# Attention and feed-forward on one core: the place of VectorE's joining adds in a group of score maxima

## The chip, the cores and the metric

One Trainium2 core runs the whole program. The metric is the device time of one execution in microseconds (us); lower is better.

## The reference, cut to what matters

```
x  = hidden states, 2048 tokens x 512, fp32
xn = layernorm(x)
q, k, v = xn @ w_qkv.T, 16 heads of 32
p  = softmax(causal(q k.T / sqrt(32)))        # per head, 2048 x 2048
x + (p v) @ w_o.T + ffn(xn)                   # ffn: fp4 weights, gate/up/down, 4096 wide
```

The change lies in the softmax alone. Softmax needs, for every query row, the maximum of its scores first and the sum of its exponentials at the end.

## The kernel before, in words

The program has three stages: norm and projections, attention (about 165 to 725 us of the span), output projection and feed-forward. In each, every engine has its own instruction list, executed in order, and semaphores tie the lists together.

Attention takes the 16 heads as 8 pairs (p0 to p7). For a pair, the transposed scores are made in 40 steps (a chunk of 512 queries against 128 keys, for both heads), and four steps are a group: ten groups a pair, 80 in all. A group is called here by its first step in its pair: s0, s4, ..., s36. The last group of each query chunk (s0, s8, s20, s36) lies on the diagonal; the other six (s4, s12, s16, s24, s28, s32) lie off it.

In group k the engines do this:

- TensorE (PE) makes the transposed scores of the group after (`scores_t`, L1041), eight of them, and between them plain scores (`scores`, L1013), eight "units" for maxima that a later pair of heads needs. It then adds the sums of exponentials of the group before into `p_o` (`row_sums`, L1084; off the diagonal it waits for `joined`), multiplies the group's exponentials with V (`product_v`, L1067, 32 matmuls), and only then makes the eighth unit. The units go to a ring of four banks of `p_s`: `bank_free` makes PE wait until the maximum of the unit four places back in the ring is taken. In groups with a `turn_max` (L1023), that one takes a place in the ring between unit seven and unit eight.
- ScalarE (ACT) turns the transposed scores into exponentials in `e_sb` (L819).
- VectorE (DVE) takes the maximum of each unit: `unit_max`, L902 on whole tiles, L898 where the diagonal is masked; L898 leaves a short accumulator read behind it. After the last unit of a batch of rows it joins the parts in `row_max` (`join_parts`, L909). Groups have eight units up to the last pair; from s12 of the last pair on there are none.
- GpSimd (POOL) adds the exponentials of two steps into `e_sum` (L736), two heads by two pairs of steps: four adds a group off the diagonal. Its order in group k is: the last two adds of group k, the first two of group k + 1, then the splitting of a batch of row maxima into three bf16 parts (`split`, L751 to L759; it waits for `row_max`), then in some groups a `normalise` (L770, in s12, s16, s24 and s28 of pairs 2, 4 and 6, and of the last).
- Off the diagonal DVE then adds the two halves of those sums (`join_sums`, L957): one add for each head, 128x512 fp32, both inputs in SBUF. It first waits for POOL's four adds of the group. Two of the joined buffers come free with it: POOL's last two adds of the following group wait for `joined`, where that group is also off the diagonal.

DVE's order in a group, before:

```
for n in units:
    if n == units[-1]:
        join_sums(k)
    unit_max(n)
    ...join_parts where a batch of rows ends
sum_steps(k)
if not units:
    join_sums(k)
```

A batch of rows ends, and `join_parts` follows, behind the sixth unit in s8, s12, s20 and s32.

Of the kernel before, what the change touches and what calls it, by code (L numbers as in the profile page):

```python
# [348 lines left out]
def attention(nc, qk_scratch, v_scratch, sum_scratch, rsum_scratch, wo_t, wo_sb, attn_t, xn_hi, xn_lo, e_sb, wv_hi, wv_lo, p_v,  # L349
# [14 lines left out]
    S_BUFS = 4  # L364
# [37 lines left out]
    def units_of(k):  # L402
        return list(range(unit_end[k - 1] if k else FIRST, unit_end[k]))
# [18 lines left out]
    for k in range(NG):  # L422
        units = units_of(k)
# [10 lines left out]
    for k in range(NG):  # L434
        diag = DIAG[GS * k % NS]
        if diag:
            ADDS.append([(a, a, 1, 0) for a in range(2)] + [(a, a, i, None) for i in (2, 3) for a in range(2)])
        else:
            ADDS.append([(2 * j + a, a, 2 * j + 1, 2 * j) for j in range(2) for a in range(2)])
        first_sum.append(len(sum_group))  # L440
        sum_group += [k] * (2 if diag else 4)
        for i, (m, a, _, _) in enumerate(ADDS[k]):
            vector = not units_of(k) and (a == 1 if diag else m >= 2)
            by_vector += vector
            by_pool += not vector
            made[k, i] = (vector, by_vector if vector else by_pool)
        added_to.append((by_pool, by_vector))

    def used_up(g, a):
        k, j = divmod(g, GS)  # L450
        return made[k, max(n for n, (_, b, y, x) in enumerate(ADDS[k]) if b == a and j in (x, y))]
# [8 lines left out]
    with ExitStack() as ctx:  # L460
# [102 lines left out]
        def exps_for(k, i):  # L563
            _, a, y, _ = ADDS[k][i]
            return (GS * k + y) * PIECES + a + 1
# [320 lines left out]
        def _(dve):  # L886
# [3 lines left out]
            def unit_max(n):  # L890
                a, i, b, w = UNITS[n % NU]
                part = max_part[:, a, i, b:b + 1]
                dve.wait_ge(scored, n + 1)
                if b == i // 4:
                    m = MASKED_UNITS.index(n)
                    if m >= 2:
                        dve.wait_ge(maxed, MASKED_UNITS[m - 2] + 1)
                    nc.vector.tensor_tensor_reduce(out=masked_scores[:, m % 2, 0:w], in0=p_s[:, slot[n] % S_BUFS, 0:w],  # L898
                                                   in1=score_mask[:, W - w:], scale=1.0, scalar=NO_MAX, op0=ALU.add,
                                                   op1=ALU.max, accum_out=part).then_inc(maxed, 1)  # L900
                else:
                    nc.vector.reduce_max(part, p_s[:, slot[n] % S_BUFS, 0:w], AX.X).then_inc(maxed, 1)  # L902

            def join_parts(p, r):
                tiles = slice(4 * r, 4 * r + 4)
                dve.wait_ge(maxed, p * NU + UNITS_TO[r])
                if p:
                    dve.wait_ge(max_split, (p - 1) * TC + r + 1)
                nc.vector.reduce_max(row_max[:, :, tiles], max_part[:, :, tiles, 0:r + 1], AX.X).then_inc(row_maxed, 1)  # L909

            def invert_sums(p):
                dve.wait_ge(sums_loaded, 16 * (p + 1))
                if p:
                    dve.wait_ge(rsums_out, 16 * p)
                nc.vector.reciprocal(rcompact[:, :], compact[:, :]).then_inc(sums_inverted, 1)

            def divide(qc):

                p, c = PAIRS - 1, (PAIRS - 1) * TC + qc
                if qc == TC - 1:  # L920
                    dve.wait_ge(rows_done, NG)
                    o = p_o[:, :, :]
                else:
                    dve.wait_ge(o_copied, c + 1)
                    o = o_sb[:, c % 2, :, :]
                dve.wait_ge(maxed, NUNIT)
                if qc:
                    dve.wait_ge(divided, 4 * qc)
                nc.vector.reciprocal(recip[:, 0:HALF], o[:, 1, :]).then_inc(inverted, 1)
                dve.wait_ge(inverted, qc + 1)  # L930
                for a in range(2):
                    for h in range(2):
                        rows = slice((2 * a + h) * D, (2 * a + h + 1) * D)
                        nc.vector.tensor_tensor(attn_rows(p, a, qc)[:, h * HALF:(h + 1) * HALF], o[rows, 0, :],
                                                recip[rows, 0:HALF], ALU.mult).then_inc(divided, 1)

            def sum_steps(k):
                for i in range(len(ADDS[k])):
                    vector, count = made[k, i]
                    if vector:  # L940
                        dve.wait_ge(exp_done, exps_for(k, i))
                        free, earlier = needs(k, i)
                        if free:
                            dve.wait_ge(*free)
                        if earlier:
                            dve.wait_ge(vector_summed, earlier)
                        nc.vector.tensor_tensor(*operands(k, i), ALU.add).then_inc(vector_summed, 1)

            def join_sums(k):
                if DIAG[GS * k % NS]:  # L950
                    return
                dve.wait_ge(pool_summed, added_to[k][0])
                if added_to[k][1]:
                    dve.wait_ge(vector_summed, added_to[k][1])
                for a in range(2):
                    other, here = ((first_sum[k] + 2 * j + a) % SUM_BUFS for j in range(2))
                    nc.vector.tensor_tensor(e_sum[:, here, :], e_sum[:, here, :], e_sum[:, other, :],  # L957
                                            ALU.add).then_inc(joined, 1)
# [6 lines left out]
            for k in range(NG):  # L965
                p, s = divmod(GS * k, NS)
                if p and s == 8:
                    invert_sums(p - 1)
                units = units_of(k)
                for n in units:  # L970
                    if n == units[-1]:
                        join_sums(k)
                    unit_max(n)
                    for p_, r in BATCHES[k]:
                        if n + 1 == p_ * NU + UNITS_TO[r]:
                            join_parts(p_, r)
# [3 lines that stand above are left out]
                if p == PAIRS - 1 and s in (20, 24, 28):  # L980
                    divide({20: 0, 24: 1, 28: 2}[s])
                if 0 < k - LAST <= KT:
                    g = k - LAST - 1
                    dve.wait_ge(wo_hi_made, g + 1)
                    nc.vector.tensor_tensor(wo_lo[:, g, :], wo_sb[:, g, :], wo_hi[:, g, :].bitcast(F32),
                                            ALU.subtract).then_inc(wo_lo_made, 1)
# [671 lines left out]
```

## Time and profile before

| | |
|---|---|
| median of 3 runs | 1799.53 us (1797.9 to 1799.81) |
| the profiled execution | 1800.45 us, its span 1798.7 us |
| PE, DVE, ACT, POOL busy in the span | 1763.6, 1237.7, 715.2, 752.2 us |
| span of attention | about 165 to 725 us |

The times in the rows below are microseconds from the start of the span; "mean" columns are nanoseconds. A row of the timeline gives start, length, engine, line, operation, output<-input and the number of merged instructions, and in brackets the idle time of the engine in front and what ended it. Neighbouring instructions of DVE overlap by some 0.08 us, so a maximum of a whole tile that is listed with 0.68 us takes 0.60 us in a sequence.

### The profile page before, as it was taken

The numbers are of one execution on the slowest core, as the hardware profiler recorded it, in microseconds if no ns is written. First come the engines' busy times: TensorE is split into PE (matmuls) and PEld (weight loads), VectorE is DVE, ScalarE is ACT, GpSimd is POOL, SyncE is SP. The second block draws the span as 40 slices with busy tenths as digits, with TensorE's granted clock in tenths as the row PEclk, the third lists the DMA queues.
The fourth block names the chain that finished last, engine by engine and source line by source line (L and its number), as shares of the span: only waits on it lengthen the run. The fifth ranks groups of instructions, "written<-read, shape, count | busy, mean of one in ns | idle before, by whom it ended". The sixth has DMA issues, their size and how long they took to land.

```text
span 1798.7 us, 28378 instructions
## 1 busy us (share of the span) xinstructions
PE 1763.6 (98%) x10176; PEld 1346.1 (75%) x10176; DVE 1237.7 (69%) x1834; ACT 715.2 (40%) x1171; POOL 752.2 (42%) x716
## 2 busy tenths in 40 slices
PE   7999999999999999999999999999999999999998
PEld 6886666656556556888888888888888888888887
DVE  5526888888888889686676567567567666666654
ACT  3324666666666665233223232323233223222322
POOL 1432888888888886122122222222222222222221
PEclk9999999999999999999999999999999999999999
DMA  8775044144143111511110110110110010010002
GB/s 280 223 230 156 10 105 84 28 105 84 29 105 83 29 40 60 182 30 36 35 35 0 35 35 0 35 35 0 35 35 14 21 35 28 7 35 0 1 1 94
DMA packets 75615, 108.55 MB, mean 60 GB/s; under 512 B 24912, under 2 KB 44992, under 8 KB 72384
## 3 DMA queue, kind: packets, MB, share of 16 engines
q1 hardware_dynamic: 75520, 107.34, 22.1%
q8 instruction: 53, 0.87, 0.2%
q14 instruction: 42, 0.34, 0.1%
HBM read 74.04 MB, written 29.59 MB: 58 GB/s over the span
## 4 chain that ended last, share of the span: by engine, by line
PE 59%; DVE 0%; ACT 0%; issue 0%; ACTq 0%
PE p_up L52 7%; PE p_v L52 7%; PE p_up L51 7%; PE p_v L51 7%; PE p_up L50 7%; PE p_v L50 7%; PE p_s L51 6%; PE p_s L52 6%; PE p_s L50 6%; PE p_s L345 0%; PE p_s L339 0%; PE p_s L340 0%; PE p_v L339 0%; PE p_v L345 0%; PE p_v L340 0%; PE p_up L339 0%
## 5 line engine op out<-in xcount | busy, mean ns | idle before, releaser
L1392 POOL TENSOR_SCALAR poly<-poly 128x1024 f32<-128x1024 f32 (+1 forms) x65 | 72.4, 1114 | 800.8 <-ACT poly L1349 800.8
L736 POOL TENSOR_TENSOR e_sum<-e_sb 128x512 f32<-128x512 f32 (+1 forms) x244 | 304.4, 1271 | 75.5 <-ACT e_sb L819 39.1
L902 DVE TENSOR_REDUCE max_part<-p_s 128x1 f32<-128x512 f32 x384 | 247.1, 683 | 62.2 <-PE p_s L1013 61.3
L819 ACT ACTIVATE e_sb<-p_v 128x512 f32<-128x512 f32 (+3 forms) x427 | 216.1, 549 | 119.6 <-PE p_v L1041 59.1
L1455 DVE SCALAR_TENSOR_TENSOR inter<-inter,gate 128x1024 f32<-128x1024 f32 (+1 forms) x65 | 78.6, 1209 | 241.1 <-ACT inter L1355 240.3
L50 PE MATMUL p_v<-xn_hi,w_hi 128*128 128x512 f32 x512 | 199.2, 389 | 0.0
L51 PE MATMUL p_v<-xn_lo,w_hi 128*128 128x512 f32 x512 | 199.2, 389 | 0.0
L52 PE MATMUL p_v<-xn_hi,w_lo 128*128 128x512 f32 x512 | 199.2, 389 | 0.0
L50 PE MATMUL p_up<-xn_hi,w_hi 128*128 128x512 f32 x512 | 199.2, 389 | 0.0
L51 PE MATMUL p_up<-xn_lo,w_hi 128*128 128x512 f32 x512 | 199.2, 389 | 0.0
L52 PE MATMUL p_up<-xn_hi,w_lo 128*128 128x512 f32 x512 | 199.2, 389 | 0.0
L1348 ACT ACTIVATE gate<-p_v 128x1024 f32<-128x1024 f32 (+1 forms) x65 | 66.0, 1015 | 332.7 <-PE p_v L52 332.7
L50 PE MATMUL p_s<-stack_hi,w_hi 128*128 128x512 f32 x504 | 196.1, 389 | 0.0
L51 PE MATMUL p_s<-stack_lo,w_hi 128*128 128x512 f32 x504 | 196.1, 389 | 0.0
L52 PE MATMUL p_s<-stack_hi,w_lo 128*128 128x512 f32 x504 | 196.1, 389 | 0.0
L1395 POOL TENSOR_TENSOR poly<-poly,gate 128x1024 f32<-128x1024 f32 (+1 forms) x65 | 179.5, 2761 | 5.4
L1067 PE MATMUL p_o<-e_sb,v_stack 128*32 128x256 f32 (+1 forms) x2304 | 149.4, 374 | 0.0
L1355 ACT ACTIVATE inter<-poly 128x1024 f32<-128x1024 f32 (+1 forms) x65 | 68.1, 1047 | 202.3 <-POOL poly L1395 202.3
L1475 DVE TENSOR_TENSOR acc<-acc,p_s 128x2048 f32<-128x2048 f32 x63 | 143.7, 2280 | 3.3 <-PE p_s L52 3.3
L898 DVE CUSTOM_DVE_ANT_0 recip<-p_s,score_mask 128x128 bf16<-128x128 f32 (+3 forms) x256 | 115.8, 485 | 37.2 <-PE p_s L1013 36.4
L819 ACT ACTIVATE e_sb<-p_st 128x512 f32<-128x512 f32 (+2 forms) x213 | 117.3, 551 | 58.2 <-PE p_st L1041 30.3
L1360 ACT ACTIVATE stack_hi<-inter 128x1024 fp32r<-128x1024 f32 (+1 forms) x65 | 68.1, 1048 | 163.0 <-DVE inter L1461 163.0
(190 smaller groups left out, 3486.7 us busy)
## 6 DMA issues: line engine op xcount, KB each, us to landing
k_stack<-qk_scratch SPq DMA_DIRECT2D x42, 256.0 KB, 7.6
qk_scratch<-out_hi SPq DMA_DIRECT2D x32, 256.0 KB, 2.6
qk_scratch<-out_lo SPq DMA_DIRECT2D x32, 256.0 KB, 3.3
q_stack<-qk_scratch SPq DMA_DIRECT2D x24, 256.0 KB, 6.5
xn_lo_scratch<-xn_lo SPq DMA_DIRECT2D x4, 1024.0 KB, 5.2
v_stack<-in_gate_up_s SPq DMA_DIRECT2D x64, 64.0 KB, 2.3
xn_lo<-xn_lo_scratch SPq DMA_DIRECT2D x4, 1024.0 KB, 13.8
scales<-in_gate_up_s SPq DMA_DIRECT2D x64, 64.0 KB, 2.5
```

The lines of the kernel that those rows point to most:

```text
L50: nc.tensor.matmul(out, w_hi, x_hi, start=first, stop=False)
L51: nc.tensor.matmul(out, w_hi, x_lo, start=False, stop=False)
L52: return nc.tensor.matmul(out, w_lo, x_hi, start=False, stop=last)
L736: nc.gpsimd.tensor_tensor(*operands(k, i), ALU.add).then_inc(pool_summed, 1)
L819: nc.scalar.activation(e_sb[:, x % E_BUFS, 0:w], bank_st(x)[:, 0:w], ACT.Exp, scale=SCALE).then_inc(exp_done, 1)
L898: nc.vector.tensor_tensor_reduce(out=masked_scores[:, m % 2, 0:w], in0=p_s[:, slot[n] % S_BUFS, 0:w], in1=score_mask[:, W - w:], scale=1.0 ...
L902: nc.vector.reduce_max(part, p_s[:, slot[n] % S_BUFS, 0:w], AX.X).then_inc(maxed, 1)
L1067: last = nc.tensor.matmul(p_o[(2 * a + h) * D:(2 * a + h + 1) * D, 0, first - h * HALF:], v_stack[p % PB][:, kt, a, :], e_sb[:, (g * PIECE ...
L1392: nc.gpsimd.tensor_scalar(part_of(poly, h, parts), part_of(poly, h, parts), GELU_A, 1.0, ALU.mult, ALU.add).then_inc(poly_done, 1)
L1395: nc.gpsimd.tensor_tensor(part_of(poly, h, parts), part_of(poly, h, parts), part_of(gate, h, parts), ALU.mult).then_inc(poly_done, 1)
L1455: nc.vector.scalar_tensor_tensor(part_of(inter, h, parts), part_of(inter, h, parts), 1.0, part_of(gate, h, parts), ALU.add, ALU.mult).then ...
L1475: nc.vector.tensor_tensor(here, here, p_out[:, :, :], ALU.add).then_inc(added, 1)
```

## The change

DVE's two joining adds of a group off the diagonal stand in front of the fifth unit's maximum (`S_BUFS` is 4), where they stood in front of the last's. Groups on the diagonal have no joining adds, and groups without units keep theirs where they were. No operation is added or taken away.

```
--- before.py
+++ after.py
@@ -968,7 +968,7 360.18 0.44 PE L1013 MATMUL p_s<-k_stack,q_stack 96*128 96x384 f32 x1
...
427.50 0.45 PE L1013 MATMUL p_s<-k_stack,stack_lo 96*128 96x384 f32 x1
                     invert_sums(p - 1)
                 units = units_of(k)
                 for n in units:
-                    if n == units[-1]:
+                    if n == units[min(S_BUFS, len(units) - 1)]:
                         join_sums(k)
                     unit_max(n)
                     for p_, r in BATCHES[k]:
```

## Rows read from the trace of the kernel before

**Rows 1.** The page: busy time of the engines in the span.

```profile
PE 1763.6 (98%) x10176; PEld 1346.1 (75%) x10176; DVE 1237.7 (69%) x1834; ACT 715.2 (40%) x1171; POOL 752.2 (42%) x716
```

**Rows 2.** Groups of instructions, attention: the joining adds.

```profile
L957 DVE TENSOR_TENSOR e_sum<-e_sum 128x512 f32<-128x512 f32 x96 | 106.3, 1146 | 1.0 <-POOL e_sum L736 0.2
```

**Rows 3.** Waits in attention: engine line <- releaser: us, times, longest.

```profile
PEld p_s L1013 <- DVE max_part L902: 6.7, 16, 0.8
...
POOL e_sum L736 <- DVE e_sum L957: 5.2, 4, 1.3
...
PEld p_s L1013 <- DVE max_part L898: 4.5, 7, 0.9
...
PE p_s L1013 <- DVE max_part L898: 3.3, 7, 0.7
```

**Rows 4.** Timeline of DVE, pair 3, s12 and s16.

```profile
398.54 0.69 DVE L898 CUSTOM_DVE_ANT_0 recip<-p_s,score_mask 128x512 bf16<-128x512 f32 x1
...
399.88 0.17 DVE L909 TENSOR_REDUCE row_max<-max_part 128x8 f32<-128x8 f32 x1
...
400.56 1.32 DVE L957 TENSOR_TENSOR e_sum<-e_sum 128x512 f32<-128x512 f32 x2
...
404.15 0.69 DVE L902 TENSOR_REDUCE max_part<-p_s 128x1 f32<-128x512 f32 x1 [0.26 <-PE p_s L1013]
...
406.66 2.10 DVE L957 TENSOR_TENSOR e_sum<-e_sum 128x512 f32<-128x512 f32 x2
```

**Rows 5.** Timeline of POOL, pair 3, s12, s16 and (414 on) s20.

```profile
395.71 5.02 POOL L736 TENSOR_TENSOR e_sum<-e_sb 128x512 f32<-128x512 f32 x4
400.66 0.70 POOL L751 CAST max_cols<-row_max 128x8 bf16<-128x8 f32 x1
...
402.72 2.51 POOL L736 TENSOR_TENSOR e_sum<-e_sb 128x512 f32<-128x512 f32 x2
...
414.27 0.23 POOL L751 CAST max_cols<-row_max 128x8 bf16<-128x8 f32 x1
...
415.42 0.22 POOL L759 CAST max_cols<-rest 128x8 bf16<-128x8 f32 x1
```

**Rows 6.** Timeline of PE: the eighth unit of s16, pair 3.

```profile
408.58 0.50 PE L1013 MATMUL p_s<-k_stack,stack_lo 96*128 96x512 f32 x1
```

**Rows 7.** Timeline of POOL, pair 2, between s12 and s16.

```profile
334.75 1.28 POOL L770 TENSOR_TENSOR acc<-acc,rsum_rows 128x512 f32<-128x512 f32 x1
336.17 2.51 POOL L736 TENSOR_TENSOR e_sum<-e_sb 128x512 f32<-128x512 f32 x2
```

**Rows 8.** Timeline of DVE and of PE, pair 2, s16.

```profile
338.71 2.10 DVE L957 TENSOR_TENSOR e_sum<-e_sum 128x512 f32<-128x512 f32 x2
...
340.40 0.50 PE L1013 MATMUL p_s<-k_stack,q_stack 96*128 96x512 f32 x1
```

**Rows 9.** Timeline of DVE, s24 of pair 2, then s24, s28, s32 of pair 3.

```profile
350.08 1.89 DVE L902 TENSOR_REDUCE max_part<-p_s 128x1 f32<-128x512 f32 x3
351.89 3.45 DVE L957 TENSOR_TENSOR e_sum<-e_sum 128x512 f32<-128x512 f32 x2
...
418.27 1.89 DVE L902 TENSOR_REDUCE max_part<-p_s 128x1 f32<-128x512 f32 x3
420.08 1.66 DVE L957 TENSOR_TENSOR e_sum<-e_sum 128x512 f32<-128x512 f32 x2
...
426.33 3.23 DVE L957 TENSOR_TENSOR e_sum<-e_sum 128x512 f32<-128x512 f32 x2
...
434.38 2.33 DVE L957 TENSOR_TENSOR e_sum<-e_sum 128x512 f32<-128x512 f32 x2
```

**Rows 10.** Timeline of POOL, pair 3: first two adds of s32, during s28.

```profile
426.05 2.97 POOL L736 TENSOR_TENSOR e_sum<-e_sb 128x512 f32<-128x512 f32 x2 [1.60 <-PE p_o L1084]
```

**Rows 11.** Timeline of PE: the eighth unit of s28, pair 2, then pair 3.

```profile
360.18 0.44 PE L1013 MATMUL p_s<-k_stack,q_stack 96*128 96x384 f32 x1
...
427.50 0.45 PE L1013 MATMUL p_s<-k_stack,stack_lo 96*128 96x384 f32 x1
```

More of the change, by code:

```diff
@@ L970, in _ @@
                 for n in units:
-                    if n == units[-1]:
+                    if n == units[min(S_BUFS, len(units) - 1)]:
                         join_sums(k)
```

## The prediction

> **What bounds the kernel now.** The page first: PE is busy 98% of the span, DVE 69%, POOL 42% [rows 1]. The change touches attention only, so the question is what PE waits for there. The table of waits for that stretch says: units waiting for a maximum of DVE, 6.7 + 4.5 us in front of weight loads and 3.3 us in front of matmuls, 14.5 us in the listed rows; and POOL waiting 5.2 us, four times, for the joining adds [rows 3]. No wait of PE behind the joining adds stands there for groups with units: where they stand, in front of the eighth maximum, they use time in which DVE has nothing else, since PE makes the eighth unit only behind 32 product matmuls. The bound is a loop in which PE, ACT, DVE and POOL hand work round within about 7 us a group, and the timelines of single groups decide, not the shares.
>
> **What is moved.** Nothing is removed or added. 43 of the 48 groups off the diagonal have units, so 86 of the 96 joining adds move, from in front of the eighth maximum to in front of the fifth: the fifth, sixth and seventh maximum now come after the pair of adds, and with them `row_max` in s12 and s32. DVE waits in order, so three things count: is POOL done with its four adds when DVE gets there; how long does the pair take there; and who waits for the fifth, sixth and seventh maximum and for `row_max`.
>
> **The price of a pair.** The 96 adds average 1.15 us [rows 2], but a pair takes 1.32 us in s12, 1.66 in s24 of pair 3, 1.84 in s4, 2.10 in s16, 2.33 in s32, 3.23 in s28, 3.45 in s24 of pair 2 [rows 4, 8, 9]. The long ones run beside POOL's own adds, and POOL's two adds there take 2.97 us [rows 10] against 2.51 alone [rows 5]: they take turns. In s12 POOL's four adds from 395.71 on take 5.02 us: the last two of s12 to about 398.2, then the first two of s16 to 400.7 [rows 5]. Before, the pair came at 400.56, when POOL was through. After, it comes at 398.54, in the middle of them [rows 4, 5]. The bounds are 1.32 (its own row) and 3.45 us; I take 3.2, because the position matches s28's.
>
> [...]
>
> **s12 and s16, pairs without `normalise` (0, 1, 3, 5), by pair 3.** The pair of adds ends at 398.54 + 3.2 = 401.74. From the fifth maximum's start to the end of `row_max` it was 400.05 - 398.54 = 1.51 us [rows 4], so `row_max` is there at 403.25 instead of 400.05. Before, the split began at 400.66, behind POOL's adds. Now POOL stands idle until 403.35. A split takes, undisturbed, 415.64 - 414.27 = 1.37 us [rows 5]: 404.72. POOL's last two adds of s16 are queued behind it, 2.51 us: 407.23, against 405.23 before. In s16 DVE finished its fourth maximum at 404.84 before [rows 4], is about 1.4 us later now, and then waits for POOL until 407.23; the pair of adds takes 2.10 us as before (its second meets POOL's next ones): 409.33. The fifth maximum of s16 (256 columns and its accumulator read) 0.42 us: 409.75. The eighth unit reuses the bank of the fifth, since `turn_max` lies between: PE starts it at 409.75, not at 408.58 [rows 6]. That is 1.2 us, and all that stands behind on PE moves with it.
>
> **The same, pairs 2, 4, 6.** They run 408.58 - 340.40 = 68.18 us in front of their like in the next pair [rows 6, 8]. `row_max` at 403.25 - 68.18 = 335.07, split to 336.5, then `normalise`, 1.28 us and a gap of 0.14 [rows 7]: 337.9; two adds, 2.51: 340.4, against 338.7. Joining adds to 342.5, fifth maximum to 343.0: PE's eighth unit starts then, not at 340.40 [rows 8]: 2.6 us.
>
> **s24 to s36.** In pair 3 the pair of adds starts at 418.27 instead of 420.08, meets POOL's two adds for s28, takes 3.2 to 3.4 us and ends about 421.6; three maxima (1.81 us from 418.27 to 420.08) follow, to 423.4. The eighth maximum could start at 421.74 before, so it is 1.7 us late [rows 9]. The trace holds an experiment for that: pair 2's adds in s24 end at 355.34, which is 423.52 in pair 3's time, 1.8 us later than pair 3's, and PE's eighth unit of s28 is 360.18 + 68.18 - 427.50 = 0.86 us later [rows 9, 11]. Against this, in s32 the pair of adds should meet less of POOL's and fall from 2.33 to about 1.3 us. I take 0.9 us a pair of heads for 0, 1, 3 and 5. In pairs 2, 4 and 6 POOL is late in s24: the adds start 351.89, while the fourth maximum was through at 350.08, a wait of 1.8 us with nothing done in it, and the slack that pair 3 has is used up already [rows 9]. POOL's own lateness from s16 (1.7) is less than PE's (2.6), so some 0.9 of that wait goes. 1.0 us remains, and the shorter covers of s28 make it 1.2.
>
> **s4.** POOL is through long before, PE makes the eighth unit late: nothing. If the cover is gone, the pair's 1.84 us would be paid up to 0.3 us a time. The last pair has only its s4 with units. Diagonal groups: untouched.
>
> **Sum.** 4 x (1.2 + 0.9) + 3 x (2.6 + 1.2) = 8.4 + 11.4 = 19.8 us. The profiled execution took 1800.45 us, 0.9 above the median; on the median of 1799.53 this gives 1819.3, and I say 1819. Lower bound: the pair of adds keeps 1.32 us in s12 and 1.66 in s24; then only pairs 2, 4 and 6 lose, 338.68 + 2.10 + 0.42 - 340.40 = 0.8 and 1.0 us each, 5.4 in all: 1805. Upper bound: the split keeps its longer form (its first cast 0.70 us, the whole 2.06 from 400.66 to 402.72 [rows 5]), 0.7 more in seven pairs, the wait in s24 stays whole (0.9 in three), and 0.3 in 8 groups s4: 19.8 + 4.9 + 2.7 + 2.4 = 29.8: 1829.
>
> **Rivals.**
> *Faster.* The adds of s28 and s32 now hold back the eighth maximum, on which PE's fourth unit of the next group waits; and POOL waits 5.2 us for joined sums [rows 3]. With the adds forward, those buffers come free earlier, and in s32 they meet POOL less, 2.33 to 1.3 us in seven pairs: 7 us gained, 1792. It decides if in s12 the fifth maximum's delay stays under the wait for the eighth unit, that is, if the pair of adds there takes below about 2 us. Against it: POOL's adds lie right there [rows 5]. 0.10.
> *No difference.* PE makes the seventh unit without the fifth maximum, and waits for exponentials anyhow; the delays drown: 1799.5. For it: DVE is 69% busy. Against it: PE's eighth unit needs the fifth maximum in s16. 0.08.
> *Small loss.* The lower bound above, 1805; 0.17.
> *Forecast.* 1812 to 1829; 0.57.
> *Larger.* The delay of POOL is carried from group to group, so that s16, s20 and s24 all pay it: 2 us more in each of seven pairs, 1833 and above; 0.08.
>
> The range that leaves out most of "faster" and of "larger" is 1800 to 1832. About 0.2% (3.6 us) is what a measurement of this kernel can tell from no change: faster 0.10, same 0.08, slower 0.82.
>
> **What the profile after would show.** Joining adds (L957): more busy time than 106.3 us, by (3.2 - 1.32) x 7 and 1.6 x 4 less 1.0 x 7, about 119 us. In s12 a pair over 3 us; `row_max` over 3 us later there; a wait of POOL's L751 behind `row_max`, new in s12; a wait of DVE's L957 behind POOL's L736 in s16 and, in pairs 2, 4 and 6, in s24; a wait of PE's L1013 behind L898 in front of the eighth unit of s16. The feed-forward is unchanged. Wrong would be the prediction if the pair in s12 stayed at 1.3 us, if PE's eighth unit of s16 came as early as before, or if the waits fell below the 14.5 us of now.

## The result and the profile after

The kernel with the change takes 1814.34 us (median of 6, 1813.53 to 1815.21) against 1799.28 us before, a ratio of 1.0084 with a 95% interval of 1.0072 to 1.0096: 15.1 us slower. The prediction was 1819 us, 19.8 us slower, with a range of 1800 to 1832. (The change is the one line with `units[-1]`; in the diff under "The change", the two lines of PE with times are those of [rows 11].)

The page after, busy time of the engines, as in [rows 1]:

```profile
PE 1766.3 (97%) x10176; PEld 1347.7 (74%) x10176; DVE 1234.9 (68%) x1834; ACT 716.0 (39%) x1171; POOL 743.7 (41%) x716
```

The joining adds after, from the groups of instructions in attention, as in [rows 2]:

```profile
L957 DVE TENSOR_TENSOR e_sum<-e_sum 128x512 f32<-128x512 f32 x96 | 105.4, 1137 | 17.6 <-POOL e_sum L736 17.1
```

The waits after in attention, for [rows 3]:

```profile
POOL max_cols L751 <- DVE row_max L909: 44.7, 21, 20.1
...
PEld p_s L1013 <- DVE max_part L898: 20.0, 26, 2.8
...
DVE e_sum L957 <- POOL e_sum L736: 17.1, 10, 2.7
...
PE p_s L1013 <- DVE max_part L898: 12.0, 13, 2.3
PEld p_s L1013 <- DVE max_part L902: 11.5, 31, 0.6
...
POOL e_sum L736 <- DVE e_sum L957: 2.8, 4, 0.7
```

The adds take no more time in all than before (105.4 us for 106.3), but DVE now waits 17.1 us for POOL in front of them, where it waited 0.2. That is 1.08 us in s16 of pairs 0, 1, 3 and 5, 2.69 us in s16 and 1.56 to 1.59 us in s32 of pairs 2, 4 and 6; none of it is in s24. PE's waits for maxima grew: 4.5 to 20.0, 3.3 to 12.0 and 6.7 to 11.5 us. POOL waits 44.7 us for `row_max`, 26.4 before. POOL's wait for joined sums shrank from 5.2 to 2.8 us, and so did its wait for PE's row sums, from 30.0 to 18.5 us, since POOL comes later.

Pair 3 runs 4.8 us later than before when it begins, so 398.54 in [rows 4] answers to 403.37. DVE there, s12 and s16:

```profile
403.29 3.28 DVE L957 TENSOR_TENSOR e_sum<-e_sum 128x512 f32<-128x512 f32 x2
406.49 0.68 DVE L898 CUSTOM_DVE_ANT_0 recip<-p_s,score_mask 128x512 bf16<-128x512 f32 x1
...
407.82 0.17 DVE L909 TENSOR_REDUCE row_max<-max_part 128x8 f32<-128x8 f32 x1
...
411.87 1.29 DVE L957 TENSOR_TENSOR e_sum<-e_sum 128x512 f32<-128x512 f32 x2 [1.08 <-POOL e_sum L736]
```

POOL there, for [rows 5]:

```profile
401.78 4.24 POOL L736 TENSOR_TENSOR e_sum<-e_sb 128x512 f32<-128x512 f32 x3
408.05 0.22 POOL L751 CAST max_cols<-row_max 128x8 bf16<-128x8 f32 x1 [2.04 <-DVE row_max L909]
...
409.33 2.51 POOL L736 TENSOR_TENSOR e_sum<-e_sb 128x512 f32<-128x512 f32 x2
```

And PE: the second, third and eighth unit of s16, for [rows 6]:

```profile
407.84 0.33 PE L1013 MATMUL p_s<-k_stack,stack_lo 96*128 96x128 f32 x1 [0.28 <-DVE max_part L898]
408.64 0.50 PE L1013 MATMUL p_s<-k_stack,stack_hi 96*128 96x512 f32 x1 [0.47 <-DVE max_part L902]
...
414.38 0.50 PE L1013 MATMUL p_s<-k_stack,stack_lo 96*128 96x512 f32 x1
```

The pair in s12 takes 3.28 us, and `row_max` is 3.1 us late (407.82 for 399.88 + 4.83). POOL has a new wait of 2.04 us, its adds of s16 start 1.8 us late (409.33 for 402.72 + 4.83), and DVE waits for them. But PE is held up earlier, at the second and third unit of s16. Its eighth, 414.38 for 408.58 + 4.83 = 413.41, is 0.97 us late without a wait of its own.

DVE in s24, s28 and s32 of pair 3, and in s32 of pair 4, for [rows 9]:

```profile
423.97 2.98 DVE L957 TENSOR_TENSOR e_sum<-e_sum 128x512 f32<-128x512 f32 x2
...
431.15 1.27 DVE L957 TENSOR_TENSOR e_sum<-e_sum 128x512 f32<-128x512 f32 x2
...
437.36 1.28 DVE L957 TENSOR_TENSOR e_sum<-e_sum 128x512 f32<-128x512 f32 x2
...
510.06 2.10 DVE L957 TENSOR_TENSOR e_sum<-e_sum 128x512 f32<-128x512 f32 x2 [1.56 <-POOL e_sum L736]
```

Where the time went is told by the start of each group's first maximum on DVE, after less before, in microseconds:

| pair of heads | s0 | s16 | s20 | s24 | s28 | s0 of the next |
|---|---|---|---|---|---|---|
| 1 | 0.12 | 1.64 | 1.12 | 1.10 | 1.96 | 0.59 |
| 2 | 0.59 | 2.94 | 4.79 | 4.78 | 4.52 | 4.80 |
| 3 | 4.80 | 6.33 | 5.79 | 5.79 | 6.65 | 5.25 |
| 4 | 5.25 | 6.76 | 9.47 | 9.96 | 9.32 | 9.56 |
| 5 | 9.56 | 11.08 | 10.55 | 10.56 | 11.43 | 10.04 |
| 6 | 10.04 | 11.53 | 14.20 | 14.75 | 14.06 | 14.32 |

Pairs 0, 1, 3 and 5 lose 0.44 to 0.48 us each, 1.8 in all; pairs 2, 4 and 6 lose 4.2, 4.3 and 4.3 us, 12.8 in all. (0.8 us of pair 2's come in s8, where DVE waits 0.86 us for a DMA in front of the reciprocal of the sums; no other pair has this wait.) In pair 4, DVE and PE in s16, for [rows 8], one timeline each:

```profile
480.89 2.88 DVE L957 TENSOR_TENSOR e_sum<-e_sum 128x512 f32<-128x512 f32 x2 [2.69 <-POOL e_sum L736]
```

```profile
484.17 0.64 PE L1013 MATMUL p_s<-k_stack,q_stack 96*128 96x512 f32 x1 [2.31 <-DVE max_part L898]
484.60 0.63 PE L1041 MATMUL p_st<-stack_hi,k_stack 128*128 128x512 f32 x1
...
487.80 0.40 PE L1013 MATMUL p_s<-k_stack,q_stack 96*128 96x512 f32 x1
```

PE waits 2.31 us, and then its matmuls of 512 columns take 0.63 us instead of 0.40. Busy time by windows; the columns are the length and the busy time of PE, PEld, DVE, ACT and POOL, each with its count, then the granted clock, the share of the DMA engines and GB/s:

```profile
480.00:484.00 4.00, 1.85 (x36) 0.86 (x28) 3.11 (x3) 0.77 (x2) 3.77 (x4) 1.00 0.02 6
484.00:488.00 4.00, 3.83 (x10) 3.15 (x11) 3.09 (x11) 2.17 (x4) 3.87 (x6) 0.57 0.00 0
488.00:492.00 4.00, 4.00 (x51) 2.45 (x49) 2.91 (x8) 2.17 (x4) 3.08 (x8) 1.00 0.00 0
```

The granted clock was 0.57 in the mean of the window from 484 us: 0.5 of full speed for 3.4 us from 484.4 on, 1.00 on both sides. Pair 6 has the same 3.4 us at 0.5 in s16, from 624.3 on; pair 2, with a wait of PE of 2.30 us at the same place, has none.

### The profile page after: what moved, and what is told of

The parts are those of the page before. It is cut to its first block, busy times and chain, and to the rows that moved or that the text cites. A ratio compares the mean times of both kernels' runs of the same rounds, so it can differ in the third digit from the quotient of the medians.

```text
span 1812.9 us, 28378 instructions
## 1 busy us (share of the span) xinstructions
PE 1766.3 (97%) x10176; PEld 1347.7 (74%) x10176; DVE 1234.9 (68%) x1834; ACT 716.0 (39%) x1171; POOL 743.7 (41%) x716
## 4 chain that ended last, share of the span: by engine, by line
PE 59%; DVE 0%; ACT 0%; issue 0%; ACTq 0%
PE p_v L50 6%; PE p_up L50 6%; PE p_up L52 6%; PE p_v L52 6%; PE p_up L51 6%; PE p_v L51 6%; PE p_s L50 6%; PE p_s L52 6%; PE p_s L51 6%; PE p_s L340 0%; PE p_s L339 0%; PE p_s L345 0%; PE p_v L339 0%; PE p_v L340 0%; PE p_up L339 0%; PE p_v L345 0%
## 5 line engine op out<-in xcount | busy, mean ns | idle before, releaser
L736 POOL TENSOR_TENSOR e_sum<-e_sb 128x512 f32<-128x512 f32 (+1 forms) x244 | 308.4, 1289 | 78.3 <-ACT e_sb L819 55.7
```

Of the source, the lines that this page charges most:

```text
L736: nc.gpsimd.tensor_tensor(*operands(k, i), ALU.add).then_inc(pool_summed, 1)
```

## The experiments

In each kernel, a condition on the place of the joining adds selects groups; elsewhere they stand as before. Times of before in the same runs: 1799.33, 1798.68 and 1799.64 us for the three sets of runs. The gains and losses by group are read as in the table above, or, where PE is named, at the start of its units. The last pair has no joining adds moved behind s4, and yet its time differs from trace to trace: from its s8 on, e1, e4, e6 and e10 get 2.4 to 2.5 us back against before (in these four, its adds of s24 and s28 take 1.29 or 1.30 us each instead of 3.37 and 2.40), e5 and e8 1.2, e7 and e9 1.8, and after, e2 and e3 0.1 or less. So the losses of the pairs don't sum to the difference of the times.

**One group at a time, and the last three.**

```
-                    if n == units[min(S_BUFS, len(units) - 1)]:
+                    if n == units[S_BUFS if s == 12 else -1]:     # e1
+                    if n == units[S_BUFS if s == 16 else -1]:     # e2
+                    if n == units[S_BUFS if s >= 24 else -1]:     # e3
+                    if n == units[S_BUFS if s >= 28 else -1]:     # e4
```

*s12 alone (e1).* 

> The joining adds stand in front of the fifth maximum in s12 alone, elsewhere where they were. Theory A (two prices: the late maxima of s12 hold back PE's second to fourth unit of s16, 0.95 us in each of 7 pairs; the wait for POOL in s16 costs the rest): about +6.7 us, near 1806, PE 0.95 us later at s16 in every pair. Rival B (as predicted: all of it goes over the late row_max and POOL to the fifth maximum of s16, and only then to PE): with the adds of s16 in their old place nobody waits, 1799 to 1801.

Measured: 1806.07 us, ratio 1.004 (1.0026 to 1.0054), 6.7 us slower. The pair in s12 takes 3.25 to 3.28 us, and in every pair of heads PE comes 0.95 to 0.98 us late between the first and the eighth unit of s16, at the same place as above, though nobody waits for the joining adds of s16. (Pairs 2, 4 and 6 lose 0.9 us more in s20 and get 0.6 back in s24.) The place and the size at s16 are those of theory A; that the total agrees too is partly luck, since the pairs lose 7.9 us in the trace and the last pair gives 2.4 back. PE's second and third unit of s16, pair 3:

```profile
406.46 0.33 PE L1013 MATMUL p_s<-k_stack,stack_lo 96*128 96x128 f32 x1 [0.26 <-DVE max_part L898]
407.26 0.50 PE L1013 MATMUL p_s<-k_stack,stack_hi 96*128 96x512 f32 x1 [0.47 <-DVE max_part L902]
```

Rival B, the way that the prediction had given this delay, falls for these pairs.

*s16 alone (e2).* 

> The adds stand forward in s16 alone. Theory A: POOL is not later than before; pairs 0, 1, 3, 5 lose nothing, pairs 2, 4 and 6 wait about 2 us for POOL in front of the fifth maximum and PE's eighth unit is 0.8 us later there: +2.5 us, near 1802. Rival B says the same. Rival C (the wait in s16 is costly by itself, whatever s12 does): +9 us or more.

Measured: 1798.51 us, ratio 0.9996 (0.9987 to 1.0005), no difference, where +2.5 us was expected. The 0.82 us at the eighth unit of s16 is there in pairs 2, 4 and 6, and is given back in s28: POOL goes on while DVE and PE stand, so it is less late in s24, where the pair of adds now takes 2.57 to 2.62 us instead of 3.45.

*s24, s28 and s32 (e3).* 

> The adds stand forward in s24, s28 and s32. Theory A, read from the trace after (PE 0.5 us earlier from s24 to s36 in each pair): -3.3 us, near 1796. The prediction's term for these groups: +7.2 us, 1806.5.

Measured: 1807.3 us, ratio 1.0045 (1.003 to 1.0059), 8.0 us slower. Theory A was wrong for this one. The prediction's 7.2 us looks right, but not by its parts: pair 2 loses 1.81 us between s24 and s28, which is the wait for POOL that the prediction had priced at 1.8; pairs 2, 4 and 6 lose 2.1, 3.3 and 3.1 us in all, 4 and 6 with the granted clock at 0.5 of full speed for 3.4 and 6.8 us behind waits of PE of 1.72 and 1.70 us; pairs 0, 1, 3 and 5, priced at 0.9 us each, gain 0.1 us or less. That these groups cost nothing in the whole change goes with s12 and s16 having held DVE and PE up already: there DVE's wait in s24 is 0, here it is 1.81 us.

*s28 and s32 (e4).* 

> The adds stand forward in s28 and s32 only. Theory A: the pair in s24 keeps 1.66 us in pairs 0, 1, 3, 5, so their 0.3 us of loss at s28 goes: about -4.5 us, near 1795. If the short pairs of s28 (1.28 us in the trace after) come only because s24's adds are early, s28 keeps 3.2 us and the gain falls to 0 to -2 us.

Measured: 1808.88 us, ratio 1.0058 (1.0044 to 1.0072), 9.6 us slower, where -4.5 us was expected. Pairs 0, 1, 3 and 5 gain 0.8 us each (1.24 - 0.40 in pair 0) with both pairs of adds at 1.28 us. Pairs 2, 4 and 6 lose 5.6 us each. POOL is late in s28 there, so DVE waits for it 1.34 us and then takes 3.42 us beside its adds, PE waits 2.01 us, and the granted clock falls to 0.5. DVE, then PE, then windows of that kernel:

```profile
357.16 3.42 DVE L957 TENSOR_TENSOR e_sum<-e_sum 128x512 f32<-128x512 f32 x2 [1.34 <-POOL e_sum L736]
```

```profile
361.23 1.86 PE L1013 MATMUL p_s<-k_stack,q_stack 96*128 96x512 f32 x3 [2.01 <-DVE max_part L902]
```

```profile
360.00:364.00 4.00, 2.77 (x8) 1.77 (x9) 4.00 (x10) 0.38 (x2) 3.64 (x4) 0.67 0.00 0
364.00:368.00 4.00, 4.00 (x20) 2.87 (x23) 3.94 (x10) 1.96 (x7) 0.34 (x1) 0.50 0.12 25
368.00:372.00 4.00, 4.00 (x41) 1.64 (x36) 0.46 (x1) 1.10 (x2) 2.67 (x6) 0.55 1.01 225
```

Of pair 2's 5.6 us, 2.2 are there at the start of the first unit of s32, the stall; 3.55 more come by the eighth. In that stretch the granted clock is at 0.5 (10.2 us of it from 361.4 on); that the clock makes all of the 3.55 is not shown by a run of its own. In all, the pairs lose 13.5 us, and the last pair gives 2.5 of it back.

**The whole change without s12 (e5).** Condition `s != 12`.

> All of the change but s12, where the adds stand in front of the last maximum again. If the prices of the groups add up (s16 -0.8, s24 to s32 +8.0 by the runs so far): near 1806.5. If s12 is what the whole change costs: 1799 to 1801. If the delay in s16 hides part of the wait in s24 (as the run with s16 alone gave back its 0.8 us there in pairs 2, 4 and 6): less than the sum, 1802 to 1805.

Measured: 1802.73 us, ratio 1.0026 (1.0015 to 1.0037), 4.1 us slower. The prices don't add up: s16's delay pays for part of the wait in s24 (pair 2 loses 0.96 us there, where it lost 1.81 with s24 to s32 alone, and DVE's wait is 0.96 us for 1.81), and the granted clock stays at 1.00 in pairs 2, 4 and 6. Putting s12's adds back in their old place takes away 11 of the 15 us.

**The split behind POOL's adds (e6).** The whole change, and `split` of the rows of s12 is made one group later on POOL.

```
-                for p, r in BATCHES[k]:
+                for p, r in [t for t in BATCHES[k] if k < 0 or t[1]] + [t for t in BATCHES.get(k - 1, ()) if k > 0 and not t[1]]:
```

> The whole change, and POOL splits the row maxima of s12 one group later, so its adds of s16 are not queued behind row_max. If the chain row_max, split, adds, fifth maximum of s16 makes the 3.4 us of pairs 2, 4 and 6: that falls to about 1 us there, no fall of the clock at s20, pairs 0, 1, 3 and 5 keep their 0.95 us: -8 to -10 us against the change, near 1805. If the late maxima alone make it: no difference, 1814.

Measured: 1819.01 us, ratio 1.012 (1.0104 to 1.0135). At s16, it did what the chain says: pairs 2, 4 and 6 lose 0.96 us there, like the others, not 3.4, and the pair of adds takes 1.28 us in all of them. But the total is 4.7 us worse than with the change as it stands (20.3 us above before, for 15.1), where 8 to 10 us less was expected. The wait turns up two groups on, in s24, and in pairs 0, 1, 3 and 5 as well: its pair of adds takes 3.43 to 3.45 us everywhere. DVE in pair 4:

```profile
481.15 1.28 DVE L957 TENSOR_TENSOR e_sum<-e_sum 128x512 f32<-128x512 f32 x2
496.71 3.43 DVE L957 TENSOR_TENSOR e_sum<-e_sum 128x512 f32<-128x512 f32 x2 [2.22 <-POOL e_sum L736]
```

Behind it PE waits 2.10 us in s28 and the granted clock falls to 0.5 in pairs 2, 4 and 6, for 3.4, 6.8 and 3.4 us. A delay taken from s16 is paid in s24.

**The length of the pair in s12 (e7).** s12 alone, as in the first run, but POOL's next adds wait until DVE's are made, so that they don't meet.

```
+                    if GS * k % NS == 12 and units_of(k):
+                        pool.wait_ge(joined, JOINED_TO[k])
                     sum_steps(k + 1, slice(0, 2), products)
```

> The adds forward in s12 alone, and POOL's first two adds of s16 wait until the joining adds of s12 are made, so that both do not meet. If the length of the pair (3.25 us for 1.32) is what makes the 0.95 us of s12 alone in each pair: the pair takes 1.3 us, PE's units of s16 come as before, and the time falls from 1806 to 1799.5 to 1802 (POOL is 1.7 us later in exchange, which pairs 2, 4 and 6 may pay). If the place alone makes it: 1806 or more.

Measured: 1800.2 us, ratio 1.001 (1.0001 to 1.002). DVE and POOL of pair 3 in s12:

```profile
397.83 1.29 DVE L959 TENSOR_TENSOR e_sum<-e_sum 128x512 f32<-128x512 f32 x2
```

```profile
399.20 2.51 POOL L736 TENSOR_TENSOR e_sum<-e_sb 128x512 f32<-128x512 f32 x2 [1.60 <-DVE e_sum L959]
```

The pair takes 1.29 us in the same place, and pairs 0, 1, 3 and 5 lose nothing. So it is the meeting with POOL's adds, not the place in DVE's list, that costs 0.95 us a pair. Pairs 2, 4 and 6 lose 0.4 us for the later POOL.

**A version with the gains alone (e8).** Condition `s >= 28 and p in (0, 1, 3, 5)`.

> The adds forward in s28 and s32 of pairs 0, 1, 3 and 5 alone, where POOL has no normalise. By the trace of the run with s28 and s32 in all pairs, those four pairs gain 0.82 us each and the others lose 5.4: -3.3 us, near 1796, no fall of the clock beyond those of before. If the gain came from POOL's state behind the stalled pairs: 1799.

Measured: 1796.61 us against 1798.68, ratio 0.9992 (0.9983 to 1.0001). Within its trace the four pairs gain 0.83, 0.78, 0.85 and 0.84 us (from 1.04 us ahead of before to 4.30). Such a gain, 3.3 us or 0.18%, is at the limit of what the times can tell, and their interval doesn't exclude no change.

**How much POOL's lateness costs (e9, e10).** The `normalise` multiplies of pairs 2, 4 and 6 work on 8 columns instead of 512, which leaves part of the attention output unnormalised; once with the adds in the old place, once in the new.

```
-                nc.gpsimd.tensor_tensor(here, here, rsum_rows[rows, qc * W:(qc + 1) * W],
+                cols = W if p == PAIRS - 2 else 8
+                nc.gpsimd.tensor_tensor(here[:, 0:cols], here[:, 0:cols], rsum_rows[rows, qc * W:qc * W + cols],
```

> The kernel before, but the normalise multiplies in pairs 2, 4 and 6 work on 8 of their 512 columns (so part of the attention output is not normalised). Those pairs should then last as long as the others, 66.97 instead of 68.18 us each: -3.6 us, near 1795.5.

Measured: 1794.8 us, ratio 0.9973 (0.9961 to 0.9984), 4.8 us faster. In the trace, pairs 2, 4 and 6 are 1.2 us shorter each, as expected.

> The whole change with the same shortened normalise. If pairs 2, 4 and 6 lose 4.3 us each because POOL is late there, every pair now costs about 0.45 us: 1798.6, 3 us above the other. If they lose it for another reason: 12 us or more above the other, 1808 to 1811.

Measured: 1801.61 us, ratio to before 1.0012 (1.0003 to 1.0022), 6.8 us above the other. Between both traces, pairs 2, 4 and 6 lose 1.38, 1.37 and 1.40 us, where they lost 4.2 to 4.3; pairs 0, 1 and 3 lose 0.40 to 0.43 as ever, and pair 5 loses 1.65 with the granted clock at 0.5 for 3.4 us in s16. So POOL's lateness makes 2.9 us of the 4.3 in pairs 4 and 6, the 1.3 to 1.4 us at the lower clock included: here the granted clock stays at 1.00 in both. In pair 2, 0.8 of the 4.2 us was the wait for a DMA, which this run doesn't have either. The expected 0.45 wasn't reached; the shortened multiplies still hold their place in POOL's list, and how much of the remaining 0.9 us each is theirs stays open.

## Why the prediction was nearly right

- *The pair of adds in s12 meets POOL's.* Right. Predicted 3.2 us instead of 1.32, measured 3.28; the delay of `row_max` 3.2, measured 3.1; POOL's end of s16 2.0 us late in pair 3, measured 1.8; and 1.7 in pair 2, where pair 4 measured 1.7. That this meeting is the cause is shown by e7.
- *s12 and s16, pairs 0, 1, 3, 5.* Predicted 1.2 us, measured 0.95 to 0.97, but by another way than said. The prediction followed the chain over `row_max`, the split and POOL to the eighth unit. It had DVE 1.4 us late at the start of s16 and did not carry that to PE, whose second and third unit need the sixth and seventh maximum of s12. These hold PE for 0.96 us, and after that the chain over POOL is just covered: its pair of adds takes 1.29 us, not 2.10, because PE's row sums, for which POOL's next adds wait, are later as well: these adds start at 412.92 for 407.13 + 4.83, 0.96 us late.
- *s12 and s16, pairs 2, 4, 6.* Predicted 2.6 us by the chain, measured 3.35, 3.34 and 3.31 at the start of the eighth unit. The chain is right (with the split moved, e6, it falls to 0.96); its pair of adds takes 2.88 us for the 2.10 assumed, since it starts in the same moment as POOL's next adds (480.89 and 480.82 us in pair 4). On top come 1.3 to 1.4 us by s24 in pairs 4 and 6, where the granted clock falls to 0.5 for 3.4 us behind the wait of 2.3 us, and nothing in pair 2, where it stays at 1.00. The prediction had no term for the clock. Predicted 7.8 us for the three, measured 12.7.
- *s24 to s36: the term that was mis-sized.* Predicted "0.9 us a pair of heads for 0, 1, 3 and 5", and 1.2 for the others, 7.2 in all. Measured from s24 to the next s0: -0.5 us in pairs 0, 1, 3 and 5, 0 in pair 2, -0.4 in 4 and 6, about -2.9 in all. The comparison of pairs 2 and 3 had been made at s28's eighth unit, and the adds of s28 were left at their price: but they fell from 3.2 to 1.28 us, and those of s32 from 2.33 to 1.28 in pairs 0, 1, 3 and 5. In pairs 2, 4 and 6, DVE's wait for POOL in s24 (1.81 us when only these groups are changed, e3) was gone after s16's, where the prediction kept 1.0 of it; a wait of 1.6 us came in s32 instead, which it had not named. The busy time of all the adds, forecast at 119 us, was 105.4 for the same reason.
- *s4.* Predicted nothing, measured nothing, though its pair grew from 1.84 to 2.09 us.
- *The rivals.* The gain of shorter pairs in s32 exists (0.8 us a pair of heads in e4 and e8, where the rival had 1.0), in the four pairs without `normalise`. In the whole change the other losses outweigh it, even with s12's adds in their old place (e5, 4.1 us slower).

The errors, 5 us too little in s12 to s16 of pairs 2, 4 and 6, 10 us too much in s24 to s36 and 1 us too much in s12 and s16 of the others, offset each other in part; the total was 4.7 us off. That it came so near is in part luck.

## What to carry to other kernels

Before an operation is moved forward in an in-order list, look at what the neighbouring engine runs at the new place, not only at the wait that it leaves: here two adds of 1.3 us became 3.3 us beside GpSimd's. Follow the lateness of everything queued behind to each of its readers, the nearest first; the long chain was right and the short one came before it. And don't add up prices of groups that were changed one by one: here a stall in one group let the late engine catch up, so the next stall shrank: DVE's wait for POOL in s24 of pair 2 was 1.81 us in e3, 0.96 in e5, behind the wait in s16, and 0 in the whole change.

## What the runs showed of the hardware

- Two adds of VectorE on 128x512 fp32, both inputs in SBUF, take 1.28 us when GpSimd is idle (s32 of pair 3 after the change, at 437.36 us) and up to 3.45 us beside GpSimd's adds (s24 of pair 2 before, [rows 9]). GpSimd's two adds take 2.97 us beside a pair of VectorE's [rows 10], for 2.51 without one [rows 5]. They take turns, an instruction of each: in s12 of pair 3 after the change, GpSimd's two adds end at 404.31 and 406.01 us and VectorE's 0.56 us behind each, at 404.87 and 406.57; in s28 of pair 3 before, they end at 427.33 and 429.02, and at 427.87 and 429.57.
- The granted clock fell to 0.5 of full speed behind single waits of PE of 1.7 to 2.3 us in pairs 2, 4 and 6, and stayed there 3.4 to 10.2 us. In pairs 4 and 6 of the changed kernel this cost 1.3 to 1.4 us on top of the wait of 2.3; in e4 each of the three pairs had 10.2 us at 0.5, and pair 2 lost 3.55 us in such a stretch. It did not fall in pair 2 of the changed kernel behind a wait of 2.30 us, nor in pair 2 of e3 behind one of 1.72; in e10 it fell in s16 of pair 5 for 3.4 us with no wait of PE over 0.5 us in the 8 us before. The length of the last wait alone doesn't tell whether the clock falls.
